# An attention and mixture-of-experts block: batch loops written out, and three projection steps moved to other slots

## The reference

```
h = layernorm(x) * (1 + ca) + sa
q, k, v = split(h @ w_qkv)                  # 16 heads of 8
attn = softmax(q @ k.T / sqrt(128))         # per batch and head 512 x 512
x = x + ga * ((attn @ v) @ w_out)
h = layernorm(x) * (1 + cb) + sb
scores = softmax(h @ w_router); best two, normalised -> comb
x = x + gb * sum_e comb[:, e] * ((silu(h @ w_gate[e]) * (h @ w_up[e])) @ w_down[e])
```

## Time and profile before

| what | value |
|---|---|
| device time, three runs | 664.18 us median (663.45 to 664.81) |
| the profiled execution | 666.58 us, of which the span (first to last instruction) is 664.8 |
| busy in the span | PE 609.4, DVE 545.0, ACT 443.4, POOL 267.2 us |
| one batch of attention, from one v projection to the next | 49.28 us; 50.69 and 50.58 where a jump lies between |
| one block of the expert stage | 24.61 to 24.64 us |
| mean granted TensorE clock | 0.96 |

### The profile page before, as it was taken

How to read it: one execution, slowest core, us unless ns; L and a number is a source line. 1 busy time by engine, 2 the same in 40 slices (tenths; PEclk the granted TensorE clock), 3 DMA queues, 4 the chain that set the end, 5 groups by cost and what they waited for, 6 DMA issues and landing times.

```text
span 664.8 us, 12806 instructions
## 1 busy us (share of the span) xinstructions
PE 609.4 (92%) x3349; PEld 282.7 (43%) x3349; DVE 545.0 (82%) x1033; ACT 443.4 (67%) x843; POOL 267.2 (40%) x384
## 2 busy tenths in 40 slices
PE   4299999999999999999999999898899999999995
PEld 3112223322322322322322322226677777777773
DVE  3698889999998999998999999417788888888884
ACT  1207878878878778878778878875465555555552
POOL 4422012222222222222222212434576786786763
PEclk9757999999999999999999999979899999999997
DMA  7712604404304304304304301154244445344401
GB/s 187 178 56 61 210 4 97 131 19 97 131 20 97 129 18 97 130 19 97 129 18 97 130 19 47 50 156 142 80 129 157 129 136 149 126 142 142 133 26 32
DMA packets 49084, 65.58 MB, mean 99 GB/s; under 512 B 9544, under 2 KB 30544, under 8 KB 49040
## 3 DMA queue, kind: packets, MB, share of 16 engines
q1 hardware_dynamic: 46416, 64.32, 33.3%
q10 hardware_dynamic: 2624, 0.79, 0.5%
HBM read 47.26 MB, written 17.83 MB: 98 GB/s over the span
## 4 chain that ended last, share of the span: by engine, by line
PE 44%; issue 17%; POOL 16%; DVE 12%; ACT 6%; DMA 2%; SPq 1%; ACTq 1%; DVEq 1%; POOLq 0%
PE o_acc L1169 15%; POOL hid_lo L601 14%; PE s_row L1142 12%; PE s_col L1155 7%; DVE negmax L853 7%; ACT probs L645 4%; DVE probs L1032 2%; PE misc L1107 1%; POOL h_lo L607 1%; PE misc L1093 1%; PE misc L1090 1%; SPq L308 1%; PE misc L1123 1%; ACT oT L649 1%; PE misc L1119 1%
## 5 line engine op out<-in xcount | busy, mean ns | idle before, releaser
L853 DVE TENSOR_REDUCE negmax<-s_row 128x1 f32<-128x512 f32 x512 | 321.6, 682 | 37.9 <-PE s_row L1142 37.1
L645 ACT ACTIVATE probs<-s_col 128x512 f32<-128x512 f32 x512 | 273.6, 599 | 75.0 <-PE s_col L1155 72.0
L1142 PE MATMUL s_row<-k_stack,q_stack 64*128 64x512 bf16 x512 | 142.4, 403 | 23.8 <-DMA k_stack<-k_scr 11.0
L601 POOL TENSOR_TENSOR hid_lo<-probs,hid_hi 128x512 fp32r<-128x512 f32 x87 | 128.5, 1493 | 61.3 <-ACT hid_hi L789 61.3
L1169 PE MATMUL o_acc<-probs,v_aug 128*32 128x512 f32 x1024 | 138.1, 612 | 0.0
L1155 PE MATMUL s_col<-q_stack,k_stack 64*128 64x512 bf16 x512 | 132.3, 384 | 6.1 <-ACT probs L645 5.1
L789 ACT ACTIVATE hid_hi<-probs 128x512 fp32r<-128x512 f32 x88 | 55.6, 632 | 86.3 <-DVE probs L1032 86.0
L1142 PEld LDWEIGHTS s_row<-k_stack,q_stack 64*128 64x128 bf16 x512 | 36.0, 93 | 177.7 <-DVE negmax L853 138.5
L1032 DVE TENSOR_TENSOR probs<-probs,q_stack 128x512 f32<-128x512 f32 x56 | 62.3, 1112 | 15.6 <-POOL hid_lo L601 13.5
L509 POOL CAST negmax_parts<-negmax 128x16 bf16<-128x16 f32 x32 | 6.3, 196 | 166.9 <-DVE negmax L853 166.9
L1022 DVE TENSOR_TENSOR probs<-probs,s_col 128x512 f32<-128x512 f32 x88 | 59.6, 677 | 3.0 <-ACT probs L809 1.6
(11 more groups left out here) (134 smaller groups left out, 684.6 us busy)
## 6 DMA issues: line engine op xcount, KB each, us to landing
q_scr<-q_parts SPq DMA_DIRECT2D x48, 128.0 KB, 2.4
k_scr<-k_parts SPq DMA_DIRECT2D x48, 128.0 KB, 2.4
q_stack<-q_scr SPq DMA_DIRECT2D x8, 768.0 KB, 6.0
k_stack<-k_scr SPq DMA_DIRECT2D x8, 768.0 KB, 7.4
q_stack<-combT_scr SPq DMA_DIRECT2D x24, 256.0 KB, 3.3
k_stack<-combT_scr SPq DMA_DIRECT2D x16, 224.0 KB, 2.8
q_stack<-combT_scr SPq DMA_DIRECT2D x16, 192.0 KB, 2.8
q_stack<-combT_scr SPq DMA_DIRECT2D x16, 160.0 KB, 2.5
```

The source lines that it names most:

```text
L601: nc.gpsimd.tensor_tensor(hid_lo[k % HIDDEN][:], weighed[(par + k) % 2], hid_hi[k % HIDDEN][:], ALU.subtract).then_inc(s["hid_split"], 1)
L645: nc.scalar.activation(probs[t % 2][:, j, :], s_col[score_bank("col", u)][:], ACT.Exp, scale=INV_SCALE).then_inc(s["exp_done"], 1)
L853: nc.vector.tensor_reduce(negmax[n % 2][:, j, qc:qc + 1], s_row[score_bank("row", u)][:], AX.X, ALU.max, negate=True).then_inc(s["row_max" ...
L1142: nc.tensor.matmul(s_row[score_bank("row", u)][:], q_stack[par][at:at + KS, head // 2, P * qc:P * (qc + 1)], k_stack[par][at:at + KS, head ...
```

## The change

1. `over_batches` calls its body eight times with plain numbers: no loop, no register arithmetic, no jump, in both stages and on all engines.
2. `TASKS` becomes `schedule(b)`. In batches 1 to 5 `xT` stands in slot 14 and works for batch b + 2; in batches 1 to 6 `q` stands in slot 0 and `k` still in slot 2. Batch 0 keeps `xT`, `q`, `k` in slots 0, 1, 2 for batch 1, and has `xT` for batch 2 in slot 14. `max1` stays at slot 0, half 2.
3. The engines follow: in batches from 1 on, ACT's *middle_q* moves from slot 2 to slot 1 (ahead of that slot's exponentials), DVE's *q_rest* from slot 1 to slot 0, POOL's `normalise1` from the start of a batch to behind `normalise2`.
4. From batch 1's load on, `load_stacks` also waits until the maxima of the third group of the running batch are stored (`max_stored`).

`TURN` is not changed.

```diff
+    def schedule(b):
+        plan = {(0, 2): ("max1", b), (4, 2): ("max2", b), (8, 2): ("max3", b), (12, 1): ("max0", b + 1),
+                (3, 0): ("o0", b - 1), (4, 0): ("o1", b - 1), (5, 0): ("attnT", b - 1), (6, 0): ("proj", b - 1),
+                (8, 0): ("v", b + 1), (10, 0): ("x1T", b - 1), (11, 0): ("router", b - 1), (14, 0): ("xT", b + 2),
+                (15, 0): ("combT", b - 1)}
+        if b == 0:
+            plan.update({(0, 0): ("xT", 1), (1, 0): ("q", 1), (2, 0): ("k", 1)})
+        else:
+            plan.update({(0, 0): ("q", b + 1), (2, 0): ("k", b + 1)})
+        return {at: task for at, task in sorted(plan.items()) if 0 <= task[1] < B}
...
         def over_batches(eng, body):
-            body(0, 0, True, False)
-            with eng.Fori(0, (B - 2) // 2) as i:
-                body(2 * i + 1, 1, False, False)
-                body(2 * i + 2, 0, False, False)
-            body(B - 1, 1, False, True)
+            for b in range(B):
+                body(b, b % 2, b == 0, b == B - 1)
...
                 sp.wait_ge(s["k_stored"], 16 * STORES * (b + 1))
+                if not (isinstance(b, int) and b == 0):
+                    sp.wait_ge(s["max_stored"], 16 * (group(b - 1, 2) + 1))
...
             def body(b, par, first, last):
-                if not last:
-                    normalise1(b + 1)
+                if first:
+                    normalise1(1)
                 split_max(b, 1)
...
                     normalise2(b - 1)
+                if b + 2 < B:
+                    normalise1(b + 2)
...
             def body(b, par, first, last):
+                middle_q, middle_k = ((2, 0), (3, 0)) if first else ((1, 0), (3, 0))
...
-            REST = {(1, 2): "q", (2, 2): "k"}
...
+                rest = {(1, 2): "q", (2, 2): "k"} if first else {(0, 2): "q", (2, 2): "k"}
...
+                    name, of = schedule(b).get(at, (None, None))
+                    if name is None:
                         return
+                    free(before[1], before[0])
+                    task(of, of % 2, name)
+                    before = name, of
```

More of the change, by code:

```diff
@@ L49, in adaln_block, with misc_use @@
     LOADS = 2
[L54 to L58, removed]
+    def schedule(b):
[8 more added lines that the diff above has]
+        return {at: task for at, task in sorted(plan.items()) if 0 <= task[1] < B}
     PROJECT = ("xT", "q", "k", "v")
-    NEXT = PROJECT + ("max0",)
     OUTPUT = ("o0", "o1", "attnT", "proj", "x1T", "router", "combT")
[L62 to L81, removed]
+    BEFORE = PROJECT + ("max0",)
+    TURNS = [(b, at) for b in range(B) for at in schedule(b)]
+    def misc_use(b, at):
+        return len(BEFORE) + TURNS.index((b, at))
     def tail_use(n):
-        return len(BEFORE) + len(tasks(True, False)) + (B - 2) * len(tasks(False, False)) \
-            + len(tasks(False, True)) + n
+        return len(BEFORE) + len(TURNS) + n
     TAIL = OUTPUT
@@ L729, in _ @@
                     middle_part(0, k_parts[:, K_MID, :], k_rest, "k_rest_ready", "k_mid")
-                evacuate(misc_use(0, None, None, name), 0, 0, name)
+                evacuate(BEFORE.index(name), 0, 0, name)
                 if name.startswith("max"):
@@ L733, in _ @@
                     place_max(0, 0, int(name[3:]))
-            MIDDLE_Q, MIDDLE_K, ROUTER_EXP, FIRST_BLOCK = (2, 0), (3, 0), (12, 0), (14, 1)
+            ROUTER_EXP, FIRST_BLOCK = (12, 0), (14, 1)
             STORE_MAX = {(1, 0): 1, (5, 0): 2, (9, 0): 3, (13, 0): 0}
@@ L750, in body @@
                                 save_o(b - 1, 1 - par, NO - 1)
-                        if at == MIDDLE_Q and not last:
+                        if at == middle_q and not last:
                             middle_part(b + 1, q_parts[:, Q_MID, :], q_rest, "q_rest_ready", "q_mid")
-                        if at == MIDDLE_K and not last:
+                        if at == middle_k and not last:
                             middle_part(b + 1, k_parts[:, K_MID, :], k_rest, "k_rest_ready", "k_mid")
@@ L772, in body @@
                             evacuate(None, b - 1, 1 - par, "router")
[L773 to L776, removed]
+                        name, of = schedule(b).get(at, (None, None))
+                        if name not in (None, "router"):
+                            evacuate(misc_use(b, at), of, of % 2, name)
             over_batches(act, body)
@@ L979, in body @@
                                 row_max(b + 1, 1 - par, t + AHEAD - SLOTS, j)
-                            if (t, j) in REST and not last:
-                                evacuate(None, b + 1, 1 - par, REST[t, j])
+                            if (t, j) in rest and not last:
+                                evacuate(None, b + 1, 1 - par, rest[t, j])
                         at = (t, half)
@@ L987, in body @@
                                 ROUTE[at](b - 1)
[L988 to L991, removed]
+                        name, of = schedule(b).get(at, (None, None))
+                        if name not in (None, "q", "k"):
+                            evacuate(misc_use(b, at), of, of % 2, name)
             dve.wait_ge(s["top_const"], 1)
@@ L1208, in _ @@
             pe.wait_ge(s["mod_ready"], 3)
+            before = "max0", 0
             def body(b, par, first, last):
-                mine = tasks(first, last)
-                before = None
                 def turn(at):
                     nonlocal before
-                    name = TASKS.get(at)
-                    if name not in mine:
+                    name, of = schedule(b).get(at, (None, None))
+                    if name is None:
                         return
[L1220 to L1229, removed]
+                    free(before[1], before[0])
+                    task(of, of % 2, name)
+                    before = name, of
                 for t in range(SLOTS):
```

## The result

The changed kernel takes 669.95 us (median of 18 runs, 664.98 to 676.37); the kernel before takes 664.77 measured beside it (661.19 to 668.04). The ratio is 1.0072, with a 95% interval of 1.005 to 1.0093: slower by 0.7%, 4.8 us above the forecast and 2 us above the upper end of its range (667.9). The profiled execution took 673.38 us, with a span of 671.8 and a mean granted clock of 0.951; before, these were 666.58, 664.8 and 0.960.

The account below looks back on a forecast made before the run. No engine fills an attention batch; PE and DVE hand the bound to each other within each slot. 664.18 - 2.7 (jumps) - 1.0 (register arithmetic) + 4.7 (slots 0 and 1) = 665.2 us, range 660.2 to 667.9.

Parts of the forecast that it names:

- The jumps: Two loop jumps in attention, each lengthening a batch window by 1.41 or 1.30 us; written out, minus 2.7 us.
- Register arithmetic: Expert stage, six block meetings on DVE in loop code: minus 6 x 0.17 = 1.0 us; nothing counted in attention slots.
- xT in slot 14: Its transposes between j = 1 and j = 2 hide in PE's wait for DVE; priced at nothing, other end 0.5 us.
- The pair: Slots 0 and 1 together, batches 1 to 6: 3.53 + 4.11 = 7.64 instead of 6.85 us, plus 4.7 us in all.
- its three patterns: Slot 2 with k, batch 7's slot 1 without a task, and batch 2's late column score, used to price slots 0 and 1.
- The load's wait: Stack loads start about 1.1 us later, with some 2.5 us of cover left before slot 8; priced at nothing.
- Rivals 1 and 2: Pair stays near 6.85 us, 660.5 to 662.0 (chance 0.25); or max1 does not wait but middle_q counts, 663.8 (0.12).
- Rival 3: What stops ACT at the jump comes again in straight code, so the 2.7 us stay: 667.9 us, chance 0.12.
- Rival 4: Late loads are missed in slot 8, costing seven batches beyond 2.5 us of delay: 667.3 for 2.8, chance 0.06.
- What would show it: Equal windows near 50.1 us, max1 held by q_rest, slot 1 hole over 1.5 us released by ACT, expert blocks 24.45.

Follow-up runs that it names:

- the product in the hole: Changed kernel plus q's own product repeated, unread, on PE in slot 1's hole in batches 1 to 6; 663.65 us, ratio 0.9992 to the kernel before.
- the old table written out: Kernel before with only its loops written out: xT, q, k in slots 0, 1, 2, no load wait; 658.4 us, ratio 0.9911 to the kernel before.

## Why the prediction was wrong

**The step that failed** is the last of the part on slots 0 and 1: "Behind the pair all engines wait at the start of slot 2 as they did, so the rest of the batch should keep its times." All durations of PE were taken from rows at a granted clock of 1.00, and the working did not ask whether PE's new hole would leave it there. No rival held this either. In its place the runs show a fall to 1.2 GHz behind the hole, 1.57 us a batch (51.07 against 49.50 with the product in the hole), in five batches of the profiled run: 7.85 us. The six experiments that put work into the hole or took the hole away have no fall in batches 1 to 6 of their profiled runs; the three that leave it open have two, three and five. With the changed kernel that is 15 falls in 24 batches with an open hole, and none in 36 without one.

The wide spread fits this: the changed kernel's runs range over 11 us, and the longer ones are those with the lower mean clock (665.20 us at 0.964, 676.37 at 0.946).

**The steps one by one.** *The jumps* were right: written out, the long windows are gone. By an estimate from the figure of the Trainium skill that was weighed there (Advanced Engine Details and Errata, Control Flow Timing), 2.5 us of them would have stayed; the windows disagree. *Register arithmetic* was mis-sized: a block takes 24.51 us and not 24.45, which gives 6 x 0.11 = 0.7 instead of 1.0, but each of the six attention batches that ran in the loop loses 0.68 us when it is written out, and I had put that at nothing, with PE's wait for DVE as its cover. The wait was no cover. In slot 9, for one, ACT's copy of the maxima starts 0.12 us behind the end of its transpose in the loop (177.73 against 177.37 + 0.24) and 0.03 us behind it written out (176.68 against 176.41 + 0.24). No run takes out the register arithmetic alone, so that it is this part of writing out is argued, not shown. *xT in slot 14* was put at nothing and gave 0.25 a batch. *The pair* was forecast well from its three patterns, 7.64 against 7.53, with some luck (slot 0 came out 0.08 above, slot 1 0.19 below). But its base moved: with q in slot 1 and all else as changed, the pair takes 2.87 + 3.51 = 6.38. So q's move costs 49.50 - 48.35 = 1.15 us a batch, and not 0.79. *The load's wait* hides as said. On an ordinary batch: 49.28 - 0.68 - 0.25 + 1.15 + 1.57 = 51.07; this holds by construction, since each term is the difference between the windows of two kernels measured. Over the program: jumps -2.7, blocks -0.7, arithmetic 6 x -0.68 = -4.1, xT 6 x -0.25 = -1.5, q's move 6 x 1.15 = +6.9, five falls +7.85, in sum +5.8 us; the two profiled executions differ by 6.8, the medians by 5.2. Not in the sum is the end of attention, with 13.65 us at the low clock in the changed kernel's profile and 6.83 in that of before. Without the five falls the sum is -2.1, and the kernel with the product in the hole came out level with before (-0.3).

**The rivals.** Rivals 1 and 2 did not come: `max1` waits, and the pair is not short. Rival 3, whatever stops ACT at the jump coming again, is excluded by the 48.60 us of the old table written out; its number (667.9) was the nearest to the result, but for another reason. Rival 4 did not come; slot 8 is not held up.

**What would show it.** The windows did have one length, but 51.07 us and not 50.1; `max1` was held, slot 14 stayed as said and the blocks nearly so (24.51 for 24.45). The hole is there, but split, with DVE as the releaser of its larger part.

The Trainium skill (TensorE: Matmul & The Clock Gate, Loop structure matters more than you think) puts it down to the loop nest whether matmuls stay at the full clock. The traces agree: two programs with the same products take 49.50 and 51.17 us a batch, by where one of them stands. Its sketch marks a wait for DMA as harmful, and DVE's copy out of the bank as not, with the next matmuls following immediately. Here they do not follow: PE waits for DVE and ACT (1.16 and 0.24 us), and the clock fell behind these waits, neither of which is for a DMA.

## What to carry to other kernels

A product that stands in a hole of PE is not only cheap there (q cost 0.37 us in slot 1): it may be what holds TensorE's clock (1.57 us a batch here), and the price of moving it out does not show in the busy times of before. When a change empties a hole on PE, give the low clock a place among the rivals, priced from rows at 1.2 GHz (a `weigh` of 1.93 us instead of 1.07), and look at the granted clock in the windows first when a result is off. Unread work in the hole is a quick way to find out, and cost nothing here: the slot took 3.92 us with it and without.

## What was not expected of the hardware

- A hole of 1.16 us brings the low clock in one batch and not in the next, with the same instructions ahead (the profiled run with *middle_q* in slot 2: two of six batches). What decides between them is not shown.
- In the changed kernel the low stretches begin 51.2 us apart (154.95, 206.15, 257.35, 308.55, 359.75), and a batch with a fall is 51.07 us long. So each of them begins at nearly the same place behind its hole, right at its end in batch 2 and 0.5 us behind it in batch 6. That may be why there are five in a row; that it is the cause was not tried.
- The end of attention has such falls in nine of the eleven profiled runs here, of 3.41 to 17.07 us. Of the two without one, one has two more row scores a slot there and the other has not; and a kernel with the same added scores had a fall. Runs of one kernel lie several us apart (655.49 to 660.44 with the old table written out), and six of them tell little about differences under 2 us.
